# Residuals and two value projections in the first step of a layer, sums by single columns, bias columns copied by ScalarE, and a new order up to the first step

## The reference

```python
def _cross_attention(q_in, kv_in, wq, bq, wk, bk, wv, bv, wo, bo, bias_k, bias_v):
    qh = (q_in @ wq + bq).reshape(b, q_len, H, K)
    kh = (kv_in @ wk + bk).reshape(b, t, H, K)
    vh = (kv_in @ wv + bv).reshape(b, t, H, K)
    kh = jnp.concatenate([kh, jnp.broadcast_to(bias_k, (b, 1, H, K))], axis=1)
    vh = jnp.concatenate([vh, jnp.broadcast_to(bias_v, (b, 1, H, K))], axis=1)
    logits = jnp.einsum('bqhk,bthk->bhqt', qh, kh) / scale
    weights = jax.nn.softmax(logits, axis=-1)
    ctx = jnp.einsum('bhqt,bthk->bqhk', weights, vh).reshape(b, q_len, H * K)
    return ctx @ wo + bo
...
x = res + _cross_attention(layer_norm(x), ...)    # twice
return x + gelu(layer_norm(x) @ w_fc1 + b_fc1) @ w_fc2 + b_fc2
```

## Time and profile before

| | us |
|---|---|
| median of 3 runs | 529.5 (527.91 to 531.82) |
| the profiled execution | 530.64 |
| its span, first to last instruction | 528.8 |
| mean granted clock of TensorE, share of full speed | 0.98 |

### The profile page before, as it was taken

How to read it: one execution, slowest core, us unless ns; L and a number is a source line. 1 busy time by engine, 2 the same in 40 slices (tenths; PEclk the granted TensorE clock), 3 DMA queues, 4 the chain that set the end, 5 groups by cost and what they waited for, 6 DMA issues and landing times.

```text
span 528.8 us, 10857 instructions
## 1 busy us (share of the span) xinstructions
PE 500.2 (95%) x3217; PEld 450.4 (85%) x3217; DVE 424.1 (80%) x864; ACT 327.8 (62%) x699; POOL 411.1 (78%) x375
## 2 busy tenths in 40 slices
PE   7988999999999999998878999999999999999787
PEld 5866899999999999987866899999989898989687
DVE  3997798897989798783689879898988888974784
ACT  3474767676767767574258676757576767676332
POOL 3767698989898989868466698988989898987620
PEclk9998999999999999999799899999999999999799
DMA  8339676767666676612107668685867676600101
GB/s 273 120 115 248 197 193 197 196 199 199 184 205 179 204 205 198 180 42 61 59 9 250 180 200 219 198 215 164 236 179 220 185 204 193 187 23 1 42 0 41
DMA packets 54180, 84.65 MB, mean 160 GB/s; under 512 B 6010, under 2 KB 34830, under 8 KB 54158
## 3 DMA queue, kind: packets, MB, share of 16 engines
q1 hardware_dynamic: 54158, 84.38, 55.1%
HBM read 54.47 MB, written 29.88 MB: 160 GB/s over the span
## 4 chain that ended last, share of the span: by engine, by line
PE 77%; DVE 11%; POOL 4%; issue 2%; DMA 2%; ACT 1%; SPq 1%; ACTq 0%; POOLq 0%; DVEq 0%
PE ring L1087 57%; PE acc L1087 10%; PE ps_ctx L1087 9%; DVE row_max L807 2%; DMA spill<-blocks 1%; DVE z_sb L844 1%; DVE total L816 1%; POOL v_lo L385 1%; DMA wf_lo<-spill 1%; POOL x_res L380 1%; SPq L263 1%; DVE v_sum L762 1%; DVE h_lo L863 1%; DVE bn L833 1%; DVE blocks L779 1%
## 5 line engine op out<-in xcount | busy, mean ns | idle before, releaser
L385 POOL TENSOR_TENSOR v_lo<-v_sum,v_hi 128x512 fp32r<-128x512 f32 x64 | 83.0, 1300 | 8.0 <-ACT v_hi L541 7.8
L392 POOL TENSOR_SCALAR probs<-probs,inv 128x512 f32<-128x512 f32 x80 | 55.4, 697 | 41.2 <-DVE inv L819 41.2
L807 DVE TENSOR_REDUCE row_max<-ring 128x1 f32<-128x512 f32 x110 | 73.3, 683 | 11.7 <-PE ring L1087 11.5
L583 ACT ACTIVATE probs<-ring,shift 128x512 f32<-128x512 f32 x110 | 74.7, 681 | 4.5 <-DVE shift L812 4.2
L779 DVE STREAM_TRANSPOSE blocks<-probs 128x512 f32<-128x512 f32 x112 | 72.7, 687 | 0.4
L1087 PE MATMUL ring<-pT_lo,v_hi 128*128 128x256 f32 x208 | 60.6, 291 | 11.4 <-DVE pT_lo L792 6.8
L397 POOL TENSOR_TENSOR pT_lo<-wf_lo,pT_hi 128x1024 fp32r<-128x1024 f32 x28 | 66.9, 2409 | 0.0
L528 ACT ACTIVATE k_hi<-ring,cols 128x512 fp32r<-128x512 f32 x57 | 37.9, 688 | 36.9 <-PE ring L1087 36.8
L1087 PE MATMUL ring<-pT_hi,v_hi 128*128 128x256 f32 x208 | 59.9, 288 | 0.0
L1087 PE MATMUL ring<-pT_hi,v_lo 128*128 128x256 f32 x208 | 59.8, 288 | 0.0
L1087 PE MATMUL ring<-wv_lo,cT_hi 128*128 128x256 f32 x192 | 54.0, 281 | 1.9 <-DVE o_lo L800 1.9
(11 more groups left out here) (171 smaller groups left out, 1674.3 us busy)
## 6 DMA issues: line engine op xcount, KB each, us to landing
spill<-blocks SPq DMA_DIRECT2D x56, 512.0 KB, 2.9
wf_hi<-spill SPq DMA_DIRECT2D x112, 128.0 KB, 3.5
wf_lo<-spill SPq DMA_DIRECT2D x112, 128.0 KB, 3.5
wk_raw<-wk_in SPq DMA_DIRECT2D x17, 256.0 KB, 2.7
wq_raw<-wq_in SPq DMA_DIRECT2D x17, 256.0 KB, 3.7
wv_raw<-wv_in SPq DMA_DIRECT2D x16, 256.0 KB, 3.9
vrows<-vrows_in SPq DMA_DIRECT2D x16, 256.0 KB, 4.1
wo_raw<-wo_in SPq DMA_DIRECT2D x16, 256.0 KB, 2.7
```

The source lines that it names most:

```text
L385: pool.tensor_tensor(v_lo[:, 2 * m:2 * m + 2, :], v_sum[:, m % 2, :].rearrange("p (t c) -> p t c", c=PW), v_hi[:, 2 * m:2 * m + 2, :].bitc ...
L392: pool.tensor_scalar(probs[:, u, q, :], probs[:, u, q, :], inv[:, u, q:q + 1], 0.0, ALU.mult, ALU.add).then_inc(p_ready_pool, 1)
L583: act.activation(probs[:, u, q, :], ring[S_BANKS[where][QTB * u + q]][:], ACT.Exp, bias=shift[:, u, q:q + 1], scale=SCALE, accum_out=row_s ...
L807: dve.reduce_max(row_max[:, u, q:q + 1], ring[S_BANKS[where][QTB * u + q]][:], AX_X).then_inc(max_done, 1)
```

## The change

1. **residual(layer)** moves from behind last_step on POOL into the layer's first_step, between normalise(2) and value_rest(2).
2. **Value projections 2 and 3** of a layer's first pair, their sums, rounding and rests, move from the prologue into first_step, on all four engines. Scores (0, 0) now wait for two sums instead of four.
3. **inverse_sums** adds the two columns by two tensor_scalar with the term as a per-partition scalar, in place of one scalar_tensor_tensor.
4. **copy_cols** moves from DVE to ScalarE, as an activation with Copy, with a semaphore cols_moved; no_cols is gone.
5. **Order up to the first step.** stats(0, 0) and stats(0, 1) run on DVE ahead of split_c(2); the inverse deviations are first in POOL's prologue, and inverse_deviation(layer + 1, 0) is inside last_step, ahead of next_wv. K tile 0 begins with the products of the rounded parts (first_keys). K tile 3 comes after the first transposes of z.
6. **Order in the first step.** DVE, instead of POOL, makes pT_lo of unit 0, and POOL that of unit 1, at the end of its first step. Banks and waits follow. step and last_step keep their order but for the columns' copy and a few waits.

```diff
-S_BANKS = {"first": [5, 4, 3, 2, 5, 0, 1, 3], "step": [0, 1, 3, 4, 1, 2, 5, 0], "last": [0, 1, 3, 4, 2, 3, 4, 5]}
+S_BANKS = {"first": [5, 1, 3, 2, 0, 1, 4, 2], "step": [0, 1, 3, 4, 1, 2, 5, 0], "last": [0, 1, 3, 4, 2, 3, 4, 5]}
...
-V_BANKS = {"step": [5, 4, 0, 2], "last": [5, 0, 1, 3], "prologue": [1, 4, 3, 5], "between": [3, 2, 4, 5]}
-K_BANKS = {"first": [4, 5, 3, 4], "step": [1, 3, 1, 3], "last": [2, 2, 1, 5], "prologue": [0, 1, 2, 3]}
-Q_BANKS = {"first": [2, 1], "step": [3, 4], "prologue": [0, 2], "between": [0, 1]}
+V_BANKS = {"first": [None, None, 3, 4], "step": [5, 4, 0, 2], "last": [5, 0, 1, 3], "prologue": [3, 5], "between": [3, 0]}
+K_BANKS = {"first": [1, 2, 4, 5], "step": [1, 3, 1, 3], "last": [2, 2, 1, 5], "prologue": [5, 4, 0, 1]}
+Q_BANKS = {"first": [0, 3], "step": [3, 4], "prologue": [2, 4], "between": [2, 4]}
...
                 first = PAIRS * layer
                 if layer == 0:
+                    inverse_deviation(0, 0)
+                    inverse_deviation(0, 1)
                     value_bias(0)
-                    inverse_deviation(0, 0)
                     split_wv(0)
-                    inverse_deviation(0, 1)
                     split_wq(0)
                     pool.wait_ge(k_filled, NK)
                     split_wk(1)
                 else:
-                    inverse_deviation(layer, 0)
+                    inverse_deviation(layer, 1)
                     pool.wait_ge(k_filled, NK * (first + 1))
                     split_wk(first + 1)
-                    inverse_deviation(layer, 1)
-                for m in range(NV):
-                    value_rest(first, m)
+                value_rest(first, 0)
+                value_rest(first, 1)
...
                 normalise(pair, 2, [0, 1])
+                residual(layer)
+                value_rest(pair, 2)
+                next_wq(pair)
                 next_wv(pair)
-                next_wq(pair)
-                moved_rest(pair, layer, 0)
+                value_rest(pair, 3)
+                moved_rest(pair, layer, 1)
...
                 value_rest(pair, 3)
+                inverse_deviation(layer + 1, 0)
...
                 step(pair, 0)
             last_step(PAIRS - 1, 0)
-            pool.wait_ge(out_rows_loaded, LOAD)
-            residual(0)
             split_mlp(0)
...
             last_step(ALL_PAIRS - 1, 1, final=True)
-            residual(1)
             split_mlp(2)
-            inverse_deviation(LAYERS, 0)
             split_mlp(3)
...
+            def copy_cols(pair):
+                act.wait_ge(k_split, NK * (pair + 1))
+                act.activation(cols[:].rearrange("p g h -> p (g h)"),
+                               step_cols[:, bass.ds(pair + 1, 1), :, :].rearrange("p n g h -> p (n g h)"), ACT.Copy).then_inc(cols_moved, 1)
...
             def prologue(layer):
                 first, where = PAIRS * layer, PROLOGUES[layer]
+                round_h(layer, 0)
+                round_v(first, 0)
                 if layer == 0:
-                    round_v(first, 0)
-                    round_h(layer, 0)
                     round_h(layer, 1)
                     round_v(first, 1)
-                    round_q(first, 0, where)
-                    round_v(first, 2)
                 else:
-                    round_h(layer, 0)
-                    round_v(first, 0)
                     round_v(first, 1)
                     round_h(layer, 1)
-                    round_v(first, 2)
-                    round_q(first, 0, where)
+                copy_cols(first)
+                round_q(first, 0, where)
                 round_q(first, 1, where)
-                round_v(first, 3)
...
                 exponential(pair, 1, 1, "first", layer, first=True)
                 normalise(pair, 1, [0])
-                round_q(pair + 1, 0, "first")
                 exponential(pair, 2, 0, "first", layer, first=True)
                 exponential(pair, 2, 1, "first", layer, first=True)
-                round_k(pair + 1, 0, "first")
+                act.wait_ge(cols_moved, pair + 1)
+                round_q(pair + 1, 0, "first")
                 exponential(pair, 3, 0, "first", layer, first=True)
                 exponential(pair, 3, 1, "first", layer, first=True)
+                round_v(pair, 2)
+                normalise(pair, 3, [0])
+                round_k(pair + 1, 0, "first")
+                normalise(pair, 3, [1])
                 round_k(pair + 1, 1, "first")
+                round_moved(pair, layer, 0, first=True)
+                round_k(pair + 1, 2, "first")
+                round_v(pair, 3)
+                round_k(pair + 1, 3, "first")
                 round_q(pair + 1, 1, "first")
-                normalise(pair, 3, [0, 1])
-                round_k(pair + 1, 2, "first")
-                round_k(pair + 1, 3, "first")
-                round_moved(pair, layer, 0, first=True)
                 round_moved(pair, layer, 1, first=True)
...
             def step(pair, layer):
                 round_moved(pair - 1, layer, 2)
+                copy_cols(pair)
                 exponential(pair, 0, 0, "step", layer)
+                act.wait_ge(cols_moved, pair + 1)
...
             def inverse_sums(pair, u):
                 dve.wait_ge(exp_done, NS * pair + QTB * (u + 1))
-                dve.scalar_tensor_tensor(out=total[:, u, :], in0=row_sum[:, u, :], scalar=1.0, in1=p_learned[:, u, :],
-                                         op0=ALU.mult, op1=ALU.add).then_inc(total_done, 1)
+                for q in range(QTB):
+                    added = dve.tensor_scalar(total[:, u, q:q + 1], row_sum[:, u, q:q + 1], p_learned[:, u, q:q + 1], 0.0, ALU.add, ALU.add)
+                added.then_inc(total_done, 1)
...
                 first, where = PAIRS * layer, PROLOGUES[layer]
                 if layer == 0:
-                    dve.wait_ge(x_loaded, LOAD)
-                    stats(0, 0)
-                    stats(0, 1)
-                    split_k(first, 0, "prologue")
                     standardise(0, 0)
-                    split_k(first, 1, "prologue")
-                    split_k(first, 2, "prologue")
-                    split_k(first, 3, "prologue")
-                    standardise(layer, 1)
+                    split_k(0, 0, where)
+                    standardise(0, 1)
+                    split_k(0, 1, where)
+                    scale_h(0, 0, where)
+                    split_k(0, 2, where)
+                    split_k(0, 3, where)
+                    scale_h(0, 1, where)
+                    split_h(0, 0)
                     dve.wait_ge(wv_split, 1)
                     sum_v(0, 0, where)
-                    scale_h(0, 0, where)
-                    scale_h(0, 1, where)
-                    split_h(0, 0)
                     split_h(0, 1)
                     sum_v(0, 1, where)
-                    sum_v(0, 2, where)
                 else:
                     scale_h(layer, 0, where)
                     dve.wait_ge(wv_split, first + 1)
...
                     sum_v(first, 1, where)
                     scale_h(layer, 1, where)
                     split_h(layer, 1)
-                    sum_v(first, 2, where)
                 split_q(first, 0, where)
-                sum_v(first, 3, where)
-                copy_cols(first)
                 split_q(first, 1, where)
...
                 maximum(pair, 3, 1, "first")
                 shifts(pair, 3, 1)
+                sum_v(pair, 2, "first")
+                split_q(pair + 1, 0, "first")
+                inverse_sums(pair, 3)
+                transpose_blocks(pair, layer, 2, first=True)
+                sum_v(pair, 3, "first")
+                transpose_blocks(pair, layer, 3, first=True)
                 split_k(pair + 1, 0, "first")
-                transpose_blocks(pair, layer, 2, first=True)
-                inverse_sums(pair, 3)
-                split_q(pair + 1, 0, "first")
+                split_k(pair + 1, 1, "first")
+                split_k(pair + 1, 2, "first")
+                moved_rest(pair, layer, 0)
                 split_q(pair + 1, 1, "first")
-                split_k(pair + 1, 1, "first")
-                transpose_blocks(pair, layer, 3, first=True)
-                split_k(pair + 1, 2, "first")
                 split_k(pair + 1, 3, "first")
-                moved_rest(pair, layer, 1)
...
+            dve.wait_ge(x_loaded, LOAD)
+            stats(0, 0)
+            stats(0, 1)
             split_c(2)
             split_c(3)
...
+                out, heads, part = ring[K_BANKS["prologue"][0]][:], slice(0, HD), slice(0, CLEN)
+                pe.wait_ge(wk_rounded, 1)
+                for c in range(DC):
+                    pe.wait_ge(cT_rounded, c + 1)
+                    pe.matmul(out, wk_hi[:, c, heads], cT_hi[:, c, part], start=c == 0, stop=False)
+                for c in range(DC):
+                    pe.wait_ge(cT_split, c + 1)
+                    pe.matmul(out, wk_hi[:, c, heads], cT_lo[:, c, part], start=False, stop=False)
```

(46 more changed lines are left out.)

29 lines of the change are left out of this document (13 added, 16 removed).

## The result

| | before | after |
|---|---|---|
| median, runs beside each other | 529.88 us (4 runs, 527.91 to 531.82) | 522.26 us (4 runs, 521.59 to 523.38) |
| span of the profiled execution | 528.8 us | 521.1 us |
| mean granted clock in it | 0.980 | 0.984 |

The ratio is 0.9871, with a 95% interval from 0.9845 to 0.9896. The medians are 7.6 us apart (1.4%), the ratio says 1.3%. Four more runs of the same kernel on another occasion gave 521.74 us, ratio 0.9848 [0.9793, 0.9903]. The prediction was 516.7 us, with a range of 512.0 to 522.5. The time lies at the very edge of it: the ratio, put on the prediction's own base of 529.5 us, gives 522.7, just outside. The 12.8 us of its sum were 7.7 us in the trace. So the study is about the 5.1 us that are missing.

What follows compares the result with a forecast made beforehand. TensorE, busy 95% of 528.8 us, was taken as the bound, so only its gaps and half clock could yield time. 2.0 - 0.5 + 5.6 + 0.5 + 5.2 = 12.8 us off the 529.5 median gave 516.7 us, range 512.0 to 522.5.

Steps and rivals of the forecast that it cites:

- The sums: In each last step, single-column sums take 0.25 us instead of 2.37, gaining 0.94 us per layer; in the loops 0.
- the slower rival: Loop steps: single-column sums blocked by POOL as the z tiles are, 3.9 us a step, 564 us; chance 0.02.
- The residuals: Last steps: moving them early removes DVE's x_res wait and shortens PE's gaps; 5.6 us between layers, 5.2 at the end.
- The first prologue: Start to first maximum: with value projections and statistics removed, 25.9 instead of 27.94 us; gain 2.0 (0.5 to 3.0).
- split_h(1) at 21.7 instead of 23.4: First prologue: where DVE's added-up list ends; PE's 0.7 + 0.5 + 1.4 us and another 1.5 us follow.
- The first step of layer 0: V2 and V3 added, HBM trip still ends the stage: -0.5 us, between -1.6 (clock falls) and +0.5.
- Between the layers: Last step of layer 0 into layer 1: 7.3 us, less 1.7 for the half clock: 5.6 gained (3.0 to 7.3).
- The first step of layer 1: HBM reads land earlier, so context(0) at full clock shows in part: +0.5 us (-1.0 to +1.3).
- The end: Last step of layer 1 into the MLP: 3.43 us gap shrinks to 0.9, half clock goes; 5.2 us (3.5 to 5.7).
- the clock never falls: Rival, whole kernel: no gap long enough to bring the half clock; gain 15.9 us, 513.6 us; chance 0.27.
- The first steps did not become the bound: Rival denied here: in both layers' first steps, DVE's added work makes context(0) 2 us later; 520.7 us; chance 0.2.
- the residual was the last wait: Last steps: a rival denied this, with about 1.5 us of each gap and its half clock staying; 522.5 us; chance 0.09.

Runs made afterwards that it cites:

- the residual kernel: Kernel before the change, with only POOL's two residuals moved to the end of the first steps: 525.96 us, ratio 0.9947.
- with ScalarE's order: Changed kernel, with ScalarE's round_h(0, 1) put ahead of its round_v(0, 0) in the first prologue: 517.47 us, ratio 0.9806.
- the products of zeros: Changed kernel, with unused products of zeros on PE in its waits in the first prologue and between the layers: 518.69 us, ratio 0.9831.
- the two kernels with fillers: Unused zero products in PE's waits: in the changed kernel, both prologues, 518.69 us; in that kernel with three orders altered, between layers only, 515.58 us.
- the order of POOL between the layers: Changed kernel, with POOL's split of wk put back ahead of the second inverse deviation between the layers: 518.64 us, ratio 0.9815.
- with the sums: Kernel before the change, with both the single-column sums and the residuals moved to the first steps: 520.68 us, ratio 0.9858.
- fillers between the layers: Changed kernel with three orders altered (ScalarE's, POOL's between layers and at the end), plus zero products on PE between the layers: 515.58 us, ratio 0.9738.

## Why the prediction was wrong in its size, and where it was right

Against the forecast, 2.1 us are missing in the first prologue, 0.7 in the first step and loop of layer 0, 2.2 between the layers and 1.0 at the end, and 0.9 more came in layer 1. The step that failed is one and the same in most of this: DVE's durations were added up as if nothing came to it late and nothing that POOL does touched h_lo. What stood in its place was a wait for ScalarE's order (1.31 us), h_lo of up to 1.75 us for 0.68 beside POOL, and more half clock in the gaps that these opened.

**The sums: right, but for the size.** The tiles after, ns min/median/max:
```profile
L824 DVE TENSOR_SCALAR total<-row_sum,p_learned x128: 200/204/218, 30.8 to 475.5; 128x1 f32<-128x1 f32 x128
...
L594 ACT ACTIVATE cols<-step_cols x16: 189/190/198, 23.5 to 458.0; 128x6 f32 x12, 128x6 f32<-128x6 f32 x4
...
L852 DVE TENSOR_SCALAR z_sb<-x_sb,mean_var,rstd x12: 405/752/1461, 11.2 to 494.8; 128x256 f32<-128x256 f32 x12
```
One column takes 200 to 218 ns instead of the 110 to 160 forecast, and the pair 0.33 us where the sum had 0.2, so the 64 sums fill 21.0 us, not 13, of the 33.0 before (shift has its operands as constants; this one reads a column). None is blocked, in any of 128, beside the same POOL that stretched the old form to 2373 ns: the slower rival is out. The columns on ScalarE are the 0.2 us predicted.

**The residuals: right, in part without saying why.** No wait for x_res, and V0 follows the last step's first outputs by 24.85 us, forecast 25.3, before 32.5. The move alone would not have done it, as the residual kernel shows; the order of rstd, which the prediction's chain doesn't mention, made it right.

**The first prologue: wrong, -0.1 instead of 2.0 us.** The step that failed is "split_h(1) at 21.7 instead of 23.4" and what follows at "0.7 + 0.5 + 1.4 us" and 1.5. It ended at 22.37, and from there to the first maximum it was 5.6 us, forecast 4.2. DVE's list was added up as if DVE never waited: ScalarE's order, plain in the diff, wasn't laid beside it (1.31 us of waiting), nor POOL's v_lo beside h_lo (0.56). DVE's list by itself was even too long: with ScalarE's order exchanged h_lo ends at 21.05, and in the changed kernel's own trace 22.37 less 1.31 and 0.56 is 20.5. Of the other 1.4 us 1.3 are the clock in the gap that this opened, which the prediction had at full level there: with ScalarE's order, and with the products of zeros too, it is 4.34 us from the end of h_lo to the first maximum instead of 5.63. With that one pair of calls exchanged the kernel takes 517.5 us.

**The first step of layer 0: sign right, -1.2 instead of -0.5.** The chain through HBM is what it was said to be: from the first maximum to context(1) 25.23 us, forecast about 25.6. Behind it the clock fell (1.7 us), the case that the text gave as the bound of -1.6.

**Between the layers: 3.4 instead of 5.6 us.** V0 came 0.5 us earlier than forecast against the last step, z of the second half 0.2 us later after V0. From there to the queries of half 1 it took 4.83 us, forecast 2.9: the mis-sized term is h_lo, twice (1.75 and 1.17 us for 0.68), with transposes at the half clock between. The second of these took 1.19 us in the kernel before already, at 267.29, so that part of the miss could have been read there. And the clock took 2.2 us behind that, where I took off 1.7. That the clock falls at this place was right.

**The first step of layer 1: 1.4 instead of 0.5 us**, 0.1 over its bound: context(1) waits 0.28 us, the gap of 1.9 us and its half clock are gone.

**The end: 4.2 instead of 5.2 us.** context(3) waits 0.77 us (forecast 0.9), o_lo 0.72 (1.0); the missing 0.9 us are h_lo beside wf_lo.

Loop steps: from context(1) of step 1 to V2 of the last step, the old o_lo wait and the half clock taken off, 174.8 us before and 174.7 after, so the sums and copies there brought nothing, as said. Of the rivals, "the clock never falls" did not happen in the profiled run; the two kernels with fillers come nearest to it. The first steps did not become the bound (25.23 us to context(1)), the residual was the last wait but for rstd, and no sum was blocked.

Left open: why gaps alike bring the half clock in one execution and not in another (below), and how much the order of POOL between the layers is worth in the total (2.5 us in the trace; 3.1 by medians across chips, 0.3 on top of ScalarE's order). V2 and V3 were not put back by themselves, so what their move costs or gives is known only together with the order.

## What to carry to other kernels

When work moves between prologue and loop, write the lists of all engines side by side up to the first result: one engine's summed durations give its earliest time, and the order of another that feeds it decides. For each instruction on the critical chain that takes two SBUF inputs, ask what GpSimd runs at that moment; a contention found for one tile is to be asked of every other with the same kind of inputs, and moving POOL's work off one of them can put it on the next. Where a gap is closed, look whether the clock falls in the next one, and judge changes under 1% by stretches of the trace, since the clock moves the total by as much.

## What was not expected of the hardware

- A kernel's time spreads with the clock: at mean granted 0.993, 0.990, 0.984 and 0.984 the changed kernel took 518.7, 520.1, 523.4 and 523.8 us; the kernel before took 526.5 at 0.997 and 531.5 at 0.980. The profiled executions of before and after, at 0.980 and 0.984, are both from the slow end.
- A gap doesn't settle the clock. A wait of 3.44 us at the same place was followed by 3.4 us of half clock in the kernel of residuals alone, and by none with the sums. Before context(1) of step 1, 2.19 and 2.39 us (the changed kernel, two executions) and 2.13 us (fillers between the layers) were followed by it; 2.00, 2.42 and 2.54 us in three other kernels weren't. The Trainium skill (TensorE: Matmul & The Clock Gate, What's actually happening) calls the number of slow matmuls at a kernel's start run-variable; these rows show the like in its middle.
- A tensor_scalar of one column with a per-partition operand takes 204 ns, more than the two-column scalar_tensor_tensor undisturbed (118 ns), but none of 128 was held up by GpSimd.
